# A layer norm spread over the engines, feed-forward weights made by ACT, and a new order for the last group

## What is computed

```python
xn = _layernorm(x)                       # x: (1, 1024, 512)
qkv = xn @ w_qkv.T                       # 32 query heads, 8 key and 8 value heads of 128
scores = einsum('bskgd,btkd->bkgst', qh, kh) * scale, causal mask, softmax
s = (probs @ vh) @ w_dense.T
h = relu(s0 * (xn @ sign(k0))) * 2.0     # sign: True -> 1, False -> -1; k0..k2 are 512x512 booleans
h = relu(s1 * (ei(h) @ sign(k1))) * 2.0  # ei: the last 20% of the columns times -4
g = silu(s2 * (ei(h) @ sign(k2)))
out = x + s * g
```

## Time and profile before

| | |
|---|---|
| median of 3 runs | 927.81 us (927.2 to 929.68) |
| the profiled execution: its own time | 922.49 us |
| its span, first to last instruction | 920.8 us |
| PE, DVE, ACT, POOL busy | 898.1, 665.8, 508.6, 483.0 us |
| granted TensorE clock, mean | 0.996 |

### The profile page before, as it was taken

How to read it: one execution, slowest core, us unless ns; L and a number is a source line. 1 busy time by engine, 2 the same in 40 slices (tenths; PEclk the granted TensorE clock), 3 DMA queues, 4 the chain that set the end, 5 groups by cost and what they waited for, 6 DMA issues and landing times.

```text
span 920.8 us, 15774 instructions
## 1 busy us (share of the span) xinstructions
PE 898.1 (98%) x4196; PEld 750.2 (81%) x4196; DVE 665.8 (72%) x1159; ACT 508.6 (55%) x1080; POOL 483.0 (52%) x388
## 2 busy tenths in 40 slices
PE   7899999999999999999999999999999999999997
PEld 6788877788878888888878887887878887778886
DVE  6535778677776777777867777687767886597864
ACT  3313665476655665566647565566556754555542
POOL 5312466455663565537645565346645655356684
PEclk9999999999999999999999999999999999999999
DMA  6156867668666857477755766585847765565662
GB/s 229 57 152 203 224 145 172 157 158 207 149 150 181 222 133 181 137 200 179 167 160 156 207 149 149 164 228 134 179 125 190 202 161 132 139 192 123 145 173 92
DMA packets 215561, 152.01 MB, mean 165 GB/s; under 512 B 23664, under 2 KB 180848, under 8 KB 215536
## 3 DMA queue, kind: packets, MB, share of 16 engines
q1 hardware_dynamic: 215536, 151.71, 63.5%
HBM read 67.90 MB, written 27.39 MB: 103 GB/s over the span
## 4 chain that ended last, share of the span: by engine, by line
issue 49%; POOL 31%; PE 15%; DVE 2%; ACT 1%; DMA 1%; POOLq 1%; SPq 0%; DVEq 0%; ACTq 0%
POOL pt_lo L823 22%; POOL w_lo L844 4%; POOL wd_lo L844 4%; PE ps_m L1311 3%; PE ps_m L1187 2%; PE ps_m L1189 2%; PE ps_m L1188 2%; PE ps_s L1296 2%; PE ps_o L1187 1%; POOL v_lo L834 1%; PE ps_o L1189 1%; PE ps_o L1188 1%; PE ps_s L1188 1%; PE ps_s L1189 1%; PE ps_s L1187 1%
## 5 line engine op out<-in xcount | busy, mean ns | idle before, releaser
L823 POOL TENSOR_TENSOR pt_lo<-pt_lo,pt_hi 128x512 fp32r<-128x512 f32 x248 | 324.9, 1339 | 299.8 <-ACT pt_hi L931 299.8
L1029 DVE CUSTOM_DVE_ANT_0 ps_s<-ps_s,mask 128x32 f32<-128x32 f32 (+31 forms) x256 | 181.3, 714 | 102.5 <-PE ps_s L1189 100.9
L931 ACT ACTIVATE pt_hi<-pt_lo 128x512 fp32r<-128x512 f32 x288 | 168.8, 627 | 105.5 <-PE ps_o L1189 54.1
L892 ACT ACTIVATE prob_odd<-ps_s,small 128x160 f32<-128x160 f32 (+15 forms) x128 | 95.9, 751 | 64.5 <-DVE small L1029 61.9
L1188 PE MATMUL ps_s<-k_lo,q_hi 128*128 128x480 f32 (+15 forms) x384 | 126.9, 330 | 0.0
L1189 PE MATMUL ps_s<-k_hi,q_lo 128*128 128x480 f32 (+15 forms) x384 | 126.5, 329 | 0.0
L1187 PE MATMUL ps_m<-xn_hi,w_hi 128*128 128x512 f32 x320 | 125.4, 392 | 0.0
L1189 PE MATMUL ps_m<-xn_hi,w_lo 128*128 128x512 f32 x320 | 125.4, 392 | 0.0
L1188 PE MATMUL ps_m<-xn_lo,w_hi 128*128 128x512 f32 x320 | 125.3, 392 | 0.0
L1187 PE MATMUL ps_s<-k_hi,q_hi 128*128 128x480 f32 (+15 forms) x384 | 124.6, 324 | 0.3 <-ACT prob_odd L892 0.3
L892 ACT ACTIVATE prob_even<-ps_s,small 128x32 f32<-128x32 f32 (+15 forms) x128 | 82.4, 646 | 75.7 <-DVE small L1029 59.4
(11 more groups left out here) (121 smaller groups left out, 1507.7 us busy)
## 6 DMA issues: line engine op xcount, KB each, us to landing
pt_lo<-prob_odd SPq DMA_DIRECT2D x128, 128.0 KB, 2.7
pt_lo<-prob_even SPq DMA_DIRECT2D x128, 112.0 KB, 2.3
pt_lo<-prob_odd SPq DMA_DIRECT2D x128, 96.0 KB, 2.2
raw<-wqk SPq DMA_DIRECT2D x40, 256.0 KB, 4.4
pt_lo<-prob_even SPq DMA_DIRECT2D x128, 80.0 KB, 2.5
inv_rows<-inv SPq DMA_DIRECT2D x32, 256.0 KB, 4.2
raw<-wd SPq DMA_DIRECT2D x32, 256.0 KB, 3.9
at_lo<-inv SPq DMA_DIRECT2D x32, 256.0 KB, 3.8
```

The costliest lines, as they stand in the source:

```text
L823: pool.tensor_tensor(pt_lo[:, slot, :], pt_lo[:, slot, :].bitcast(F32), pt_hi[:, hi_slot, :], ALU.subtract).then_inc(land_lo, 1)
L892: act.activation(prob_tile(i, tile), as_tiles(score_row(i, tile)), ACT.Exp, scale=-1.0, bias=neg_max[:, slot:slot + 1], accum_out=row_sum[ ...
L931: act.activation(pt_hi[:, hi_slot, :], pt_lo[:, LAND_AT[i] + j, :].bitcast(F32), ACT.Copy).then_inc(land_hi, 1)
L1029: dve.tensor_tensor_reduce(out=scores, in0=scores, in1=mask[:, S - width(i % BLOCKS, tile):S], scale=-1.0, scalar=BIG, op0=ALU.add, op1=AL ...
```

## The change

1. Prologue: the steps of the layer norm are interleaved. `moments` is cut in two (`moments`: to var+eps; `rooted`: reciprocal and Newton step). DVE takes the next pair's statistics and the low parts between the two. The copies of `values` 0 to 3 go from DVE to ACT. PE's list has `values` 0.1 and 0.2 after blocks 2 and 3, and 0.3 after blocks 4 and 5.
2. An activation with Sqrt on one zero element stands first on ACT.
3. POOL's splits wait: `wv` 1 until two blocks are normalised, the weights q0, q2, q3 until 4, 6 and 8 are (`SPLIT_AFTER`).
4. SP issues x2 and x3 ahead of the last two `wv` loads, and x6, x7 ahead of q2. `WARM_UP` goes from 36 to 27.
5. The feed-forward weights are made by ACT, in twelve items `build.layer.c`.
6. All lists of `LAST` are replaced. The body is as it was.

```diff
-WARM_UP = 36
+WARM_UP = 27
+SPLIT_AFTER = {"q0": 4, "q2": 6, "q3": BLOCKS}
...
-    pe = ln(0, 1) + values(0, 0, 1) + ln(2, 3) + values(0, 2, 3) + unit("q0") + ln(4, 5) + unit("q1") \
-        + ln(6, 7) + unit("q2") + unit("q3") + unit("k") + values(0, 4, 5, 6, 7) \
+    pe = ln(0, 1) + values(0, 0) + ln(2, 3) + values(0, 1, 2) + ln(4, 5) + values(0, 3) + unit("q0") \
+        + ln(6, 7) + unit("q1") + unit("q2") + unit("q3") + unit("k") + values(0, 4, 5, 6, 7) \
...
-    act = hi(wv[0][0]) + root[:1] + hi(*wv[0][1:], *ln(0, 1)) + root[1:2] + hi(split[0], *ln(2, 3), split[1]) \
-        + root[2:3] + hi(split[2], *ln(4, 5), q0, split[3]) + root[3:] \
-        + hi(*ln(6, 7), q1, split[4], q2, *wv[1][:2], q3, *wv[1][2:], k)
+    act = [("root_table",)] + hi(wv[0][0]) + root[:1] + hi(*wv[0][1:], *ln(0, 1)) + root[1:2] \
+        + hi(split[0], *values(0, 0), *ln(2, 3), split[1], *values(0, 1)) + root[2:3] \
+        + hi(split[2], *values(0, 2), *ln(4, 5)) + root[3:] + hi(*values(0, 3), q0, split[3], *ln(6, 7)) \
+        + hi(split[4], q1, q2, *wv[1][:2], q3, *wv[1][2:], k)
...
-    dve = stats[0] + moments[:1] + scale[0] + lo(*ln(0, 1)) + stats[1] + moments[1:2] + scale[1] \
-        + lo(*values(0, 0), *ln(2, 3), *values(0, 1)) + stats[2] + moments[2:3] + lo(*values(0, 2)) + scale[2] \
-        + lo(*values(0, 3), *ln(4, 5), q0) + stats[3] + moments[3:] + scale[3] \
-        + lo(*ln(6, 7), q1, q2, q3, k, *values(0, 4, 5, 6, 7))
+    dve = stats[0] + moments[:1] + rooted[:1] + scale[0] + stats[1] + lo(*ln(0)) + moments[1:2] + lo(*ln(1)) \
+        + rooted[1:2] + scale[1] + stats[2] + lo(*ln(2)) + moments[2:3] + lo(*ln(3)) + rooted[2:3] + scale[2] \
+        + stats[3] + lo(*ln(4)) + moments[3:] + lo(*ln(5)) + rooted[3:] + scale[3] \
+        + lo(q0, *ln(6, 7), q1, q2, q3, k, *values(0, 4, 5, 6, 7))
...
-    sp = x[0:2] + wv_load[0] + x[2:4] + load[0:2] + x[4:6] + load[2:3] + x[6:8] + wv_load[1] \
+    sp = x[0:2] + wv_load[0][:2] + x[2:4] + wv_load[0][2:] + x[4:6] + load[0:2] + x[6:8] + load[2:3] + wv_load[1] \
...
 LAST = {
     "pe": """
-        scores.1.0 scores.1.1 scores.1.2 unit.q1.1.0 scores.1.3 scores.2.0 unit.q1.1.1 scores.2.1
+        unit.q3.1.0 scores.1.0 scores.1.1 unit.q3.1.1 scores.1.2 scores.1.3 unit.q3.1.2 scores.2.0
...
+                        if half == 0 and c == 1:
+                            pool.wait_ge(xn_ready, 2)
...
+                        if kind == "prologue" and piece in SPLIT_AFTER:
+                            pool.wait_ge(xn_ready, SPLIT_AFTER[piece])
...
+            def build_ffn_weights(r, layer, c):
+
+                slot = (K_PIECE + layer) % RAW
+                bits = raw[:, slot, :].bitcast(U8).rearrange("p (c o) -> p c o", o=E)
+                if c == 0:
+                    act.wait_ge(shared_done, max(r.shared_no(w) for w in r.order if w[0] == "unit"))
+                    if layer == 2:
+                        act.wait_ge(scores_done, SCORES * GROUPS)
+                    act.wait_ge(raw_loaded[slot], 16 * ((K_PIECE + layer) // RAW + 1))
+                scaled_part = layer > 0 and c == CHUNKS - 1
+                mul, add = (inh_mul[:, 0:1], inh_add[:, 0:1]) if scaled_part else (2.0, minus_one)
+                act.activation(ffn_w[layer][c], bits[:, c, :], ACT.Identity, scale=mul, bias=add)\
+                   .then_inc(ffn_w_built, 1)
...
+                    if what == "root_table":
+                        act.wait_ge(zero_made, 2)
+                        act.activation(zero, zero, ACT.Sqrt)
+                        continue
...
+                    elif name == "values":
+                        _, half, b = item
+                        no = r.shared_no(item)
+                        act.wait_ge(shared_done, no)
+                        act.activation(stage(half, b), bank[:, :], ACT.Copy).then_inc(shared_read, 1)
...
+            def rooted(half):
+
+                blocks = slice(half * 2, half * 2 + 2)
+                base = LN_STEPS * half
                 dve.wait_ge(ln_sqrt, half + 1)
                 dve.reciprocal(rstd[:, blocks], std[:, blocks]).then_inc(ln_step, 1)
```

166 lines of the change are left out of this document (82 added, 84 removed).

## The result

The changed kernel took 921.1 us, median of 5 runs (920.11 to 922.9), against 927.81 (927.2 to 929.68) before: ratio 0.9937, 95% interval 0.9913 to 0.996. By the medians it is 6.7 us faster, by the ratio 5.8. The profiled execution took 921.1 us, span 919.4, against 922.49 and 920.8, so the two profiles differ by only 1.4 us. The reason must be looked for before single rows are compared, since the gain of the median does not show in the ends of the profiles.

A forecast was written before the change was run, and what follows sets the result against it. PE was taken to bound the unchanged loop body, so only prologue and last group could move. -5.3 + 0.6 = -4.7 us from 922.49 gave 917.8, plus 5.3 from profile to median 923.1 us; range 918 to 927.

The forecast's parts named there:

- the 5.3 of the sum: Prologue: net gain of 5.3 us, from 7.0 us gained less 1.7 us for a fall of the clock.
- its 0.6: Last group: 0.6 us slower, with a range from 3 us faster to 4 us slower.
- the 5.3 us added: Whole kernel: the runs' median lies 5.3 us above the profiled execution, taken over from before to turn 917.8 into 923.1.
- No second wait: Prologue: after PE's 1.6 us idle piece before the first product, no wait over 0.5 us until k is read.
- The likeliest case: Prologue: the clock falls at PE's 1.6 us idle piece, costing 1.7 us (bounds 0 and 1.7).
- the 7.0 of the sum: Prologue: k read at 39.7 instead of 46.65 us, a gain of 7.0 us before any fall of the clock.
- rival (1): Clock holds in the prologue: 6.4 us faster, 9 with shorter last-group waits, 919 to 921 us; chance beyond 7 us 0.14.
- Rival (2): Prologue: clock rises late, transposes and values 0.0 at half speed, 1.7 to 2.5 us more, 925; chance 0.60 with forecast.
- 1.3 lost in two waits: Last group: PE waits 1.9 and 1.2 us for the third and fourth unit's low parts, 1.3 us lost against before.
- 1.5 won at the builds: Last group: PE's 1.5 us wait for a feed-forward read goes, since ACT makes the chunks.
- Rival (3): Last group gives the gain back by 3 to 5 us more waits: 926 to 928 us, no difference; chance 0.18.
- (4): Last group: row 2's read lands late and stalls ACT's order; gain gone at 826, 931 us at 829; chance 0.08.

The follow-up runs named there:

- longer series: The unchanged kernel before, measured again beside the experiments in series of 16 to 29 runs: medians 925.1 to 926.0 us.
- holding alone: Kernel before plus only the waits on POOL's splits; lists, loads, table load and 36 transposes as before: 922.71 us, ratio 0.997.
- lists alone: Changed kernel without early table load, held splits, new load order or shorter warm-up; interleaved prologue lists and changed last group stay: 924.19 us, ratio 0.9994.
- all but the holding: Changed kernel without the waits that hold POOL's splits of wv 1, q0, q2 and q3: 923.38 us, ratio 0.9994.
- all of the prologue: Changed prologue with the last group's lists as before and feed-forward builds on DVE: 917.6 us, ratio 0.9927 to the kernel before.

## Why the prediction was right, and where its reasons were not

**The time.** 923.1 us were predicted with a range of 918 to 927, and 921.1 measured; faster was given 0.74. The bound was named rightly: with the clock's share taken out, from the first product to the first scores PE needs 38.0 to 39.5 us in every version with the new lists, and what the edits moved lies in the two ends of the program.

That the number came within 2.0 us is in part luck, for four misses cancel. The prologue gained 1.6 us more than the 5.3 of the sum, and the last group lost 0.8 more than its 0.6. The middle took 4.1 us longer in the one profile than in the other, which the prediction had at nothing, so the changed kernel's profile took 921.1 us where 917.8 was expected. And the 5.3 us added for the distance from profile to median was not there: the changed kernel's median and its profile are both 921.1. -1.6 + 0.8 + 4.1 - 5.3 = -2.0. The 5.3 came from one profile and one median of the kernel before; against the medians of the longer series (925.1 to 926.0) the distance is 2.6 to 3.5.

**The start.** Predicted PE on x at 8.5 and the first product at 11.1 after 1.6 us of idleness; measured 8.78, 11.53 and 1.6. The held product (1.05), the `scale` (1.00), and the last of the first four `wv` loads, which ACT begins to split at about 9.6 (9.1 worked out), are nearly as worked out. What was credited was not: the prediction counted 1.3 us for the table load and the rest of 2.4 for the holding. Counted from ACT's first split, taking out the table load gives 0.53 to 0.60 us and the holding 1.95 to 2.02. The root does come 1.5 us sooner, but the steps behind it then run into POOL's first split, which ends no sooner. The prediction had worked that hold into its chain, and so came near the start; but the 1.3 us is the table load's length, and not what taking it out is worth.

The Trainium skill's page "SBUF — State Buffer", section "SBUF: two separate sides", says that VectorE instructions with two inputs in SBUF or in a 2-port mode take turns with GpSimd for one pair of ports, whole instructions at a time. The rows agree: products of 128x2 that take 0.16 alone took 1.04 and 1.19 beside POOL's splits, and each ended within 0.05 us of a split's end.

**No second wait.** Predicted nothing over 0.5 us until k; measured one of 0.45 at blocks 2 and 3, where a small step of 1.21 us at 11.89 was held by POOL's three splits, which the prediction had not priced. Blocks 4 and 5 came in time, and the reason given (DVE's relief of four copies) is not borne out: with the copies back on DVE they were in time too, if only by 0.1 us and in a profile with a fall of the clock. The waits of 1.0 and 2.6 us go with the new lists: these alone need 38.9 us from the first product, and the holding alone leaves both waits standing. As the copies' move saves no time that shows, the order of the statistics and steps on DVE is the likely reason; no run changes that order by itself.

**The clock in the prologue.** The likeliest case took 1.7 us off for a fall; in the changed kernel's profile it held, so the prologue gained 6.9 us, the 7.0 of the sum without it. This was rival (1). In nine profiles PE was on x at 8.8 to 9.7 us with the new lists, and the clock fell in four of them before or behind the first product, so taking it was fair and one trace does not settle it. Rival (2), the clock not up in time, did not come: it rose at 6.97. What neither I nor a rival had is how a fall multiplies a delay: with the splits not held, 3.3 us of delay became 5.45, and 1.4 of 6.9 us were left of the gain in that profile.

**The last group.** Predicted 0.6 us longer, by 1.3 lost in two waits and 0.8 for the reading of row 2, less 1.5 won at the builds. The profile shows 1.4 longer. The two waits came at their places, 2.2 and 1.1 (predicted 1.9 and 1.2), and the wait for row 2's landing at the first feed-forward read was 1.3 instead of 0.8. ACT made the chunks 0.64 us apart, not 0.52:

```profile
807.32 2.55 ACT L894 ACTIVATE w_hi<-raw,small 128x512 fp32r<-128x512 uint8 x4
```

That cost nothing by itself: builds on DVE gave the same length. The step that was mis-sized is the comparison with before. The old lists took 136.92, 138.52 and 137.17 us in three profiles, the changed ones 136.75 to 138.30 in eight (means 137.5 and 137.5): the change of lists is neutral, which the ratio of 1.001 says too, and 1.4 us from one pair of profiles was within that spread. Rival (3) was therefore not the case, nor (4).

**Which part carries the gain.** Holding alone 0.997, lists alone 0.9994, all but the holding 0.9994, all of the prologue 0.9927. Neither half alone is near the whole. By the checkpoints the holding alone gives 2.0 us; in the changed kernel the first product comes 1.5 us sooner, and the way from there is 5.35 us shorter: the lists take out two waits of 3.7 us and with them the 1.7 of clock behind the second one. Why the lists alone measured no gain is only partly shown: in that profile the first load landed 1.3 us later than in the profile before, and the late start with its fall of 6.83 us ate most of what the lists won; counted from ACT's first split they still gain 2.8 us there. The ratio's interval leaves room for 2.7 us, so it is not shown that the lists alone gain nothing. Whether the fall comes in most of its executions, one profile does not tell.

## What to carry to other kernels

When two engines share work at the start of a program, hold the one that nobody waits for until the chain is through: one semaphore wait turned 2.86 us into 1.00 and brought PE to its first real work 2.0 us sooner, and a kernel with all the rest of the change but without the holding measured 0.9994. Look for loads queued behind writes that are waited for in another engine's order: putting one 256 KB load and one row's write further ahead on SP took out three waits of PE (4.5 us in the profile), while twelve instructions moved between engines made no difference. And cut two traces at the same instruction before comparing their ends, since here the untouched middle differed by more than the edit of the last group.
